# Attention with 64-wide heads: the value products of two query tiles in a row in every second step, and turned weights packed by length

## What is computed

```python
B, S, H, N, D = (2, 256, 128, 16, 64)      # x has 4 x 1024 x 128 here
q, k, v = jnp.einsum('bsx,xMnd->Mbnsd', x, qkv)
a = jnp.einsum('bnsd,bntd->bnst', q, k) * q.shape[-1] ** (-0.5)
cum = jnp.cumsum(rpe_bias[:, :s], axis=-1)
rel = jnp.arange(s)[:, None] - jnp.arange(s)[None, :]
bias = jnp.where(rel >= 0, cum[:, jnp.clip(rel, 0)], PAD)
a = jax.nn.softmax(a + bias, axis=-1)
mix = jnp.einsum('bnst,bntd->bnsd', a, v)
return jnp.einsum('bnsd,ndx->bsx', mix, out_w)
```

## Time and profile before

| | us |
|---|---|
| median of 3 runs | 3110.31 |
| lowest and highest run | 3101.8, 3111.2 |
| the profiled execution | 3096.14 |
| its span from first to last instruction | 3094.4 |
| PE busy | 2468.9 (80% of the span) |
| DVE busy | 1758.3 (57%) |
| ACT busy | 1320.7 (43%) |
| POOL busy | 874.1 (28%) |

### The profile page before, as it was taken

How to read it: one execution, slowest core, us unless ns; L and a number is a source line. 1 busy time by engine, 2 the same in 40 slices (tenths; PEclk the granted TensorE clock), 3 DMA queues, 4 the chain that set the end, 5 groups by cost and what they waited for, 6 DMA issues and landing times. The chain is left out here.

```text
span 3094.4 us, 49721 instructions
## 1 busy us (share of the span) xinstructions
PE 2468.9 (80%) x16698; PEld 1426.3 (46%) x16698; DVE 1758.3 (57%) x4932; ACT 1320.7 (43%) x2638; POOL 874.1 (28%) x1043
## 2 busy tenths in 40 slices
PE   4369998999999999999936834999999865766655
PEld 2147767985776667666623522222222332222212
DVE  4446553215556665556672014888888349577574
ACT  2126664445666666566641112366666620211202
POOL 0126654434566333333323030000000004123140
PEclk8669999998999999999966866799999887878876
DMA  3231113012111000000000035101010000000000
GB/s 115 21 126 31 31 32 79 28 33 99 30 17 29 2 15 2 16 2 1 2 3 29 15 34 178 34 25 37 25 36 25 2 28 0 0 0 0 0 0 27
DMA packets 75148, 93.55 MB, mean 30 GB/s; under 512 B 10002, under 2 KB 53140, under 8 KB 73252
## 3 DMA queue, kind: packets, MB, share of 16 engines
q1 hardware_dynamic: 65188, 77.94, 8.3%
q0 software_dynamic: 9728, 12.63, 2.3%
HBM read 54.60 MB, written 35.53 MB: 29 GB/s over the span
## 5 line engine op out<-in xcount | busy, mean ns | idle before, releaser
L1020 ACT ACTIVATE WA<-a_E 128x1024 f32<-128x1024 f32 (+3 forms) x384 | 301.3, 815 | 160.4 <-PE a_E L959 123.4
L491 PE MATMUL a1b_S<-a1b_Kf,a1b_Qf 64*128 64x512 f32 (+3 forms) x1164 | 243.0, 522 | 0.0
L590 ACT COPY a1b_PT<-a1b_T 128x512 f32<-128x512 f32 (+3 forms) x288 | 153.6, 534 | 206.3 <-PE a1b_T L501 206.3
L516 PE MATMUL a1b_O<-a1b_PT,WA 128*64 128x128 f32 x3456 | 225.8, 277 | 14.8 <-ACT WA L594 14.8
L411 POOL TENSOR_SCALAR XR<-XR,a1b_rinv 128x384 f32<-128x384 f32 (+1 forms) x192 | 161.5, 852 | 268.0 <-DVE a1b_rinv L663 267.5
L935 PE MATMUL a_S<-a_KS,a_QS 54*128 54x512 bf16 (+3 forms) x768 | 204.0, 351 | 32.4 <-DVE a_mx L1056 19.8
L658 DVE COPY a1b_PT<-a1b_T 128x128 f32<-128x128 f32 (+3 forms) x288 | 140.6, 488 | 152.6 <-PE a1b_T L501 152.6
L516 PEld LDWEIGHTS a1b_O<-a1b_PT,WA 128*64 128x64 f32 x3456 | 186.0, 137 | 81.8 <-ACT a1b_PT L590 39.7
L1849 PE MATMUL a_D<-a_Sr,WA 128*128 128x512 f32 x128 | 97.7, 906 | 135.8 <-POOL a_Sr L1833 135.8
L411 POOL TENSOR_SCALAR WA<-WA,a1b_rinv 128x128 f32<-128x128 f32 (+1 forms) x194 | 121.1, 636 | 215.7 <-DVE a1b_rinv L663 215.7
L581 ACT ACTIVATE XR<-XR,a1b_nmax 128x384 f32<-128x384 f32 (+1 forms) x192 | 168.1, 881 | 3.1
(11 more groups left out here) (417 smaller groups left out, 5376.0 us busy)
## 6 DMA issues: line engine op xcount, KB each, us to landing
WA<-in_w SPq DMA_DIRECT2D x8, 1024.0 KB, 9.9
a_QS<-qstack SPq DMA_DIRECT2D x32, 216.0 KB
a_KS<-kstack SPq DMA_DIRECT2D x32, 216.0 KB
a1b_tb<-tab SPq DMA_DIRECT2D x12, 512.0 KB
qstack<-a2s_parts SPq DMA_DIRECT2D x24, 256.0 KB, 2.9
kstack<-a2s_parts SPq DMA_DIRECT2D x24, 256.0 KB, 3.6
f_slots<-f1r_zrows SPq DMA_DIRECT2D x9, 516.0 KB, 5.6
f1t_xs<-f_slots SPq DMA_DIRECT2D x9, 516.0 KB, 7.4
```

Source lines behind the costliest of these rows:

```text
L491: pe.matmul(pS[k % NB][:, 0:hi - lo], Qf[half, b0 % 2, i0 * P:(i0 + 1) * P], Kf[half, b0 % 2, lo:hi], start=True, stop=True).then_inc(s_ps, 1)
L516: ins = pe.matmul(pO[half, i % CT * P:(i % CT + 1) * P], V[s][:, j, half], PT[:, i % 2 * HG + u, j * P:(j + 1) * P], start=(j == 0), stop= ...
L590: act.copy(PT[:, i % 2 * HG + u, lo:hi], pT[0][:, 0:hi - lo]).then_inc(t_sb_a, 1)
L1020: act.activation(PT[:, q % NP, :, off:CH], pE[q % 2][:, :, off:CH], ACT.Exp).then_inc(e_sb, 1)
```

## The change

The values are no longer computed one step after their turn. In steps 2, 4 and 6 PE computes those of two tiles one after another, (0, 1), (2, 3) and (4, 5), and the last two, (6, 7), follow in step 0 of the next iteration, after its scores (after the loop for the last one). Steps 1, 3, 5 and 7 have none. The waits of `values` are the same with the iteration moved back by one where needed. ACT empties the second half of O in step 1 of the next iteration and no longer at the end of its own; the first half is still emptied in step 5. As turned weights now live a step longer, they need room for four tiles: tiles 0 and 4 go to free columns of `w1`, in which the softmax buffers of tiles i % 4 < 2 are packed by their longest use (5 and 6 blocks for a head), tiles 2 and 6 and the odd tiles to `PT`.

```diff
-    PT = ph.sb("PT", [P, 4, T])
+    PT = ph.sb("PT", [P, HG * (7 * P + T)])
...
     def soft(i, u):
 
-        return (S_low, S_high)[i % 4 // 2][:, i % 2 * HG + u, 0:length(i)]
+        if i % 4 < 2:
+            lo = (u * 5, 10 + u * 6)[i % 4] * P
+            return w1[:, lo:lo + length(i)]
+        return S_high[:, i % 2 * HG + u, 0:length(i)]
+
+    def turned(i, u, lo, hi):
+
+
+        if i % 4 == 0:
+            at = (22 + u * 5) * P
+            return w1[:, at + lo:at + hi]
+        at = HG * 7 * P + u * T if i % 2 else u * 7 * P
+        return PT[:, at + lo:at + hi]
...
-            def values(it, s, i):
+            def values(it, back, s, i):
+
                 done = turn_at[i, HG - 1, i // CT] + 1
-                pe.wait_ge(t_sb_a, it * HALF + (done + 1) // 2 + 1)
-                pe.wait_ge(t_sb_d, it * HALF + done // 2 + 1)
+                pe.wait_ge(t_sb_a, it * HALF + (back * HALF + (done + 1) // 2 + 1))
+                pe.wait_ge(t_sb_d, it * HALF + (back * HALF + done // 2 + 1))
...
                     for c in range(2):
                         scores(it, b, i + LEAD, c)
-                    if i >= 1:
-                        values(it, s, i - 1)
-                values(it, s, TT - 1)
+                    if i == 0 and not (isinstance(it, int) and it == 0):
+                        for back in (TT - 2, TT - 1):
+                            values(it, -1, 1 - s, back)
+                    if i and i % 2 == 0:
+                        for back in (i - 2, i - 1):
+                            values(it, 0, s, back)
...
                     if i == CT + 1:
                         empty(it, s, 0)
+                    if i == 1 and not (isinstance(it, int) and it == 0):
+                        empty(it, 1 - s, -1)
                     exponentials(it, i + 2)
-                empty(it, s, 1)
```

More of the change, by code:

```diff
@@ L331, in attention @@
     Qf, Kf = ph.sb("Qf", [P, 2, T]), ph.sb("Kf", [P, 2, T])
-    PT = ph.sb("PT", [P, 4, T])
-    S_low = w1.rearrange("p (n t) -> p n t", n=4)
+    PT = ph.sb("PT", [P, HG * (7 * P + T)])
     S_high = XR[:, :, :].rearrange("p (n k) d -> p n (k d)", n=4)
@@ L516, in values @@
                         ins = pe.matmul(pO[half, i % CT * P:(i % CT + 1) * P], V[s][:, j, half],
-                                        PT[:, i % 2 * HG + u, j * P:(j + 1) * P], start=(j == 0), stop=(j == i))
+                                        turned(i, u, j * P, (j + 1) * P), start=(j == 0), stop=(j == i))
                 ins.then_inc(pv_ps, 1)
@@ L560, in _ @@
             loops(pe, body)
+            for back in (TT - 2, TT - 1):
+                values(IT, -1, 1, back)
             pe.wait_ge(v_sb, IT * 2 + 2)
@@ L589, in copies @@
                         act.wait_ge(t_ps, it * R + k + 1)
-                        act.copy(PT[:, i % 2 * HG + u, lo:hi], pT[0][:, 0:hi - lo]).then_inc(t_sb_a, 1)
+                        act.copy(turned(i, u, lo, hi), pT[0][:, 0:hi - lo]).then_inc(t_sb_a, 1)
             def empty(it, s, c):
                 act.wait_ge(pv_ps, it * TT + CT * (c + 1))
+                c = c % 2
                 act.copy(mU[s][:, c * CH:(c + 1) * CH], pO[:, :]).then_inc(o_sb, 1)
@@ L619, in _ @@
             loops(act, body)
+            empty(IT, 1, -1)
         @block.vector
@@ L657, in copies @@
                         dve.wait_ge(t_ps, it * R + k + 1)
-                        dve.tensor_copy(PT[:, i % 2 * HG + u, lo:hi], pT[1][:, 0:hi - lo]).then_inc(t_sb_d, 1)
+                        dve.tensor_copy(turned(i, u, lo, hi), pT[1][:, 0:hi - lo]).then_inc(t_sb_d, 1)
             def inverse(it, i):
```

## The result

The changed kernel takes 3138.45 us (median of 6 runs, 3134.82 to 3145.03), the kernel before 3110.76 us in its 6 runs beside them. The ratio is 1.0092, with a 95% interval of 1.0070 to 1.0114: the change makes the kernel slower by 28 us. The forecast was 3139, made as +29 us.

What follows compares the result with a forecast made beforehand. PE, busy 98.15 us of 100, was taken to bound the kernel. The terms summed to +0.92 us an iteration, 32 x 0.92 = +29 us on the median of 3110.3, so 3139 us, with a range of 3122 to 3170.

Steps and rivals of the forecast that it cites:

- three groups of values fewer: On PE, four groups of values in an iteration in place of seven, each giving back 0.15 us: -0.44 us.
- wait on the emptying of O: In step 5, PE's wait for ACT to empty O before the values of tile 4 goes: -0.69 us an iteration.
- first turn of tile 6, on ACT: In step 5, PE newly waits for ACT to copy out bank 0: +0.21 us an iteration.
- second turn of tile 6, on ACT: PE newly waits for ACT's copy of the first turn, which stands behind both 1024-key exponentials: +1.51 us an iteration.
- second turn of tile 4, on DVE: At its fifth block PE newly waits for DVE's copy of bank 1, behind the biases of tile 6: +0.33 us.
- What bounds it: PE's own row of work sets the pace, busy 98.15 us of 100; other engines count only where PE waits.
- The price of a group: On PE, a group of values costs 0.15 us however long it is, plus 0.055 us for each record.
- What is late next: Values leaving step 5 uncover ACT's longest piece; new waits of +0.21 and +1.51 us at tile 6, +0.33 at tile 4.
- From ACT to PE: From the end of an ACT copy to PE takes 0.15 us; at 0.05 the stretch to tile 6's second turn shortens 0.1.
- From the sum to the time: 32 x 0.92 = +29 us, added to the runs' median of 3110.3 us: 3139 us.
- Rival (1): Faster through fewer groups and no wait, if PE's new waits stay under 1.13 us: 3074, or 3081 us; chance 6%.
- Rival (3): PE's new gap of 1.5 us makes its clock fall to half, 24 to 48 us more: 3163 to 3187; chance 15%.

Runs made afterwards that it cites:

- groups one by one again: The kernel with three moves on ACT and DVE, values of tiles 0 to 3 again one by one in steps 1 to 4; period 34.31 us against 34.01.
- the old wait alone: The kernel before, with O emptied in step 5 behind ACT's copy of head 0, nothing else; 3086.14 us against 3109.4, ratio 0.9923.
- DVE's copy moved: The changed kernel, with DVE's copy of the first turn of tile 4 ahead of the last bias of tile 6; 3126.8 us in one run.
- three moves on ACT and DVE: Changed kernel: tile 7 exponentials behind step 6's head 0 copies, O emptied earlier in step 5, DVE's tile 4 copy before tile 6's last bias; 3075.02 us, ratio 0.9889.
- the longer copy: The changed kernel with one more ACT copy of 512 columns behind the emptying of O in step 5; 3177.6 us in one run.

## Why the prediction was right

Its terms for one iteration, and what the runs showed for each in the loop of a1b:

| term | predicted, us | measured, us | from |
|---|---|---|---|
| three groups of values fewer | -0.44 | -0.45 | 0.15 for each, groups one by one again |
| wait on the emptying of O | -0.69 | -0.69 | 35.04 - 34.35, the old wait alone |
| first turn of tile 6, on ACT | +0.21 | +0.11 | 128-key scores take 0.53, without a wait 0.42 (1389.09 - 1388.67, the old wait alone) |
| second turn of tile 6, on ACT | +1.51 | +1.52 | 2.41 - 0.89 |
| second turn of tile 4, on DVE | +0.33 | +0.38 | 35.96 - 35.58, DVE's copy moved |
| sum | +0.92 | +0.87, and the period +0.92 | |

- *What bounds it.* Right: in the loop, the waits and the starts of groups that each experiment took away or added were found again in the period, to 0.06 us.
- *The price of a group.* Right, and read from two rows of the trace alone, by the difference between 24 and 60 records. The drain that the Trainium skill names in TensorEngine Tiling (Array Packing), section Key Properties, agrees with it in kind: the 0.15 goes with the number of groups and not with the records. That it is a drain, and not another cost of going from one kind of product to the next, no run shows.
- *What is late next.* Right in place and size. The copy that PE waits for began at 3.88 us after the second turn of tile 5 before and after, so the time at which PE would be let go could be read from the kernel before.
- *From ACT to PE.* The small miss, and only in half of the iterations. The 0.15 us was read from the emptying of O to the values. In the 16 looped iterations a copy and the turn behind it are 0.05 us apart (1109.13 to 1109.18), so the first wait is 0.10 shorter and the stretch up to the second turn of tile 6 took 4.51 and not 4.61 us. In the 16 written-out ones they are 0.15 apart (893.09 to 893.24), the first wait is 0.62 - 0.42 = 0.20 us, and the stretch takes 4.60, as predicted. In the loop 0.05 more on DVE and some 0.05 in the seven turns behind the wait, which take 0.91 us and not 0.86, stand against the 0.10: that the sum comes out at 0.92 there is in part luck. Where the 0.15 held, the period grew by 0.99.
- *From the sum to the time.* 32 x 0.92 = 29 us; with 0.99 in half of the iterations it would be 31. The runs gave 28, and their interval, 22 to 35 us, cannot tell these apart. The sum had to start from the median and not from the profiled execution, which was 14 us below it.
- *Rival (1)*, faster. Its point was that the new waits stay under 1.13 us in an iteration. The change alone does not reach it, but with three moves on ACT and DVE they do, and then its price holds too: 34 us gained, between the 29 that it named with the first wait kept and the 36 without.
- *Rival (3)*, the clock. It did not happen at a gap of 1.35 us, and the longer copy shows that at 1.87 to 1.90 us it happens in 16 of the 32 iterations. It was a real danger, 0.5 us away. The clock page of the Trainium skill, TensorE: Matmul & The Clock Gate, Part 1, says that the clock follows how busy PE has been; the rows agree, with 1.00 across the gap and 0.50 just behind it.

## What to carry to other kernels

When work is moved along a saturated engine, ask first what the other engines did meanwhile: their longest piece is covered by what stands on the first engine between two dependences, and that cover, not their average load of 60%, decides. Here 1.9 us of wait and values left a stretch in which ACT needs 3.9 us to come to its next copy, and the stretch shrank by 0.3 us. The repair is to put the long piece behind the short one that others wait for; and a wait that looks like the reason for a rearrangement may need only one instruction moved, as here, where the earlier emptying of O alone gave 0.8%.

## What the runs showed of the hardware

- A gap of 1.35 to 1.38 us in PE's work, once in 36 us, left the clock at 2.4 GHz all 32 times. One of 1.87 to 1.90 us brought it to 1.2 GHz in 16 of 32 iterations, for 1.6 us of lost time each.
- A group of half-width products (128 x 64 tiles) ahead of full-width ones costs 0.15 us whatever its length (34.31 against 34.01 us with two groups more). Products of 64 rows cost 0.20 us at their end whichever of the two follows (0.63 us for 256 keys before values, 1.06 us for 512 before a turn).
- From the end of an ACT copy to the turn on PE that waits for it took 0.05 us in each looped iteration and 0.15 us in each written-out one. The cause is open.
- A single stall of PE of 26 to 30 us at one place, for which the profile names no releaser, stood in nine of twelve profiles. It is as long as the whole effect that was measured here. The unchanged kernel's time differed by as much from session to session (3110 and 3082 us).
